# TensorE's order of the MLP's two layers inside a round: the second layer's unit ahead of the first layer's

## What is computed

```
normed = (xf - mu) / jnp.sqrt(var + 1e-05) * ln_g + ln_b
x_attn = normed @ attn_w.T + attn_b + xf
h = jnp.einsum('meti,ehi->meth', tok, fc1_w) + fc1_b[None, :, None, :]
h = jax.nn.gelu(h, approximate=False)
y = jnp.einsum('meth,edh->metd', h, fc2_w) + fc2_b[None, :, None, :]
out = jax.nn.gelu(yf @ next_w.T + next_b, approximate=False)
```

## Time and profile before

| | us |
|---|---|
| median of 3 runs | 179.08 |
| the three runs | 178.96, 179.08, 179.25 |
| the profiled execution, its own time | 178.95 |
| its span, first to last instruction | 177.2 |
| PE busy | 166.2 (94%) |
| DVE busy | 131.4 (74%) |
| ACT busy | 94.7 (53%) |
| POOL busy | 93.3 (53%) |

### The profile page before, as it was taken

One profiled execution on the slowest core, in us unless ns is written; L12 is line 12 of the kernel. 1 busy time (PEld: TensorE's weight loads), 2 busy tenths in 40 slices (PEclk: granted clock), 3 DMA queues, 4 the chain that ended last, 5 costly groups with the idle time before them and its releaser, 6 DMA issues.

```text
span 177.2 us, 3381 instructions
## 1 busy us (share of the span) xinstructions
PE 166.2 (94%) x1129; PEld 134.6 (76%) x1129; DVE 131.4 (74%) x406; ACT 94.7 (53%) x220; POOL 93.3 (53%) x153
## 2 busy tenths in 40 slices
PE   5987999999999999988999989999999999998992
PEld 2575776587654679856557889999999999987891
DVE  4889973785430496899875798989989897658983
ACT  3048992342223322201435765977769597786691
POOL 4227673599920000120401495896978969698600
PEclk9999999999999999999999999999999999999999
DMA  4995000000000000000000000010010100101103
GB/s 141 372 433 235 4 0 4 4 0 0 0 0 0 0 4 0 0 2 4 0 0 0 0 4 0 0 61 4 0 59 2 63 0 6 57 4 59 42 21 118
DMA packets 2326, 7.53 MB, mean 42 GB/s; under 512 B 255, under 2 KB 893, under 8 KB 2053
## 3 DMA queue, kind: packets, MB, share of 16 engines
q1 hardware_dynamic: 2162, 7.18, 10.5%
q10 hardware_dynamic: 146, 0.13, 0.2%
HBM read 5.22 MB, written 2.10 MB: 41 GB/s over the span
## 4 chain that ended last, share of the span: by engine, by line
PE 68%; DVE 10%; POOL 8%; ACT 6%; issue 5%; DMA 1%; ACTq 0%; DVEq 0%; POOLq 0%
PE bank L1184 10%; PE bank L1204 9%; PE bank L1134 7%; PE bank L995 6%; PE bank L1054 6%; PE bank L1048 5%; PE bank L1131 4%; PE bank L944 3%; PE bank L1154 3%; DVE u L713 2%; PE bank L1019 2%; POOL hid_p L472 2%; PE bank L971 2%; POOL rstd L455 2%; PE bank L1161 1%
## 5 line engine op out<-in xcount | busy, mean ns | idle before, releaser
L472 POOL TENSOR_TENSOR hid_p<-hid_f,hid_p 128x256 fp32r<-128x256 f32 x52 | 37.2, 739 | 17.8 <-ACT hid_p L605 16.2
L603 ACT ACTIVATE hid_f<-bank,pa 128x256 f32<-128x256 f32 x64 | 30.7, 488 | 17.5 <-PE bank L1184 15.7
L1184 PE MATMUL bank<-xaT_p,fc_p 128*128 128x256 f32 x192 | 35.1, 293 | 0.2 <-issue 0.2
L1204 PE MATMUL bank<-hid_p,out_hi 128*128 128x256 f32 x128 | 33.0, 292 | 1.4 <-POOL hid_p L472 1.2
L455 POOL TENSOR_TENSOR rstd<-spread,neg_half 128x8 f32<-128x8 f32 x8 | 13.2, 1646 | 37.3 <-DVE spread L849 37.3
L1184 PEld LDWEIGHTS bank<-xaT_p,fc_p 128*128 128x128 f32 x192 | 26.7, 189 | 0.3 <-issue 0.3
L1204 PEld LDWEIGHTS bank<-hid_p,out_hi 128*128 128x128 f32 x128 | 23.3, 187 | 3.2 <-POOL hid_p L472 2.4
L605 ACT ACTIVATE hid_p<-bank,pa 128x256 fp32r<-128x256 f32 x48 | 23.4, 487 | 0.0
L1134 PE MATMUL bank<-pb,xh 128*128 128x128 f32 x128 | 19.5, 275 | 0.0
L1204 PE MATMUL bank<-hid_p,out_lo 128*128 128x256 f32 x64 | 17.8, 278 | 0.0
L693 DVE BATCH_NORM_STATS2 st<-h 128x6 f32<-128x128 f32 x64 | 13.9, 279 | 4.5 <-ACT h L530 4.2
(11 more groups left out here) (130 smaller groups left out, 341.5 us busy)
## 6 DMA issues: line engine op xcount, KB each, us to landing
fc_w<-in_fc SPq DMA_DIRECT2D x2, 2048.0 KB, 11.2
out<-res SPq DMA_DIRECT2D x7, 256.0 KB, 2.0
pa<-in_pack_a SPq DMA_DIRECT2D x1, 407.0 KB, 3.2
pb<-in_pack_b SPq DMA_DIRECT2D x1, 320.0 KB, 4.4
out<-res SPq DMA_DIRECT2D x2, 128.0 KB, 1.7
pc<-in_pack_c ACTq DMA_DIRECT2D x1, 128.5 KB, 2.3
pw<-in_pack_a SPq DMA_DIRECT2D x1, 64.0 KB, 4.0
emb_w<-in_emb SPq DMA_DIRECT2D x1, 62.5 KB
```

The source lines that it names most:

```text
L472: nc.gpsimd.tensor_tensor(hid_p[1][:, half, c, :], hid_f[:, m % HID_SLOTS, :], hid_p[0][:, half, c, :].bitcast(F32), ALU.subtract).then_in ...
L603: full = nc.scalar.activation(hid_f[:, m % HID_SLOTS, :], src, ACT.Gelu, bias=bias)
L1184: last = mm(fc1_bank(8 * b + n)[:, 0:HALF], fc1_p[w][:, e * HID + c * P:e * HID + (c + 1) * P], xaT_p[m][:, b % 2, half, :], start=(k == 0 ...
L1204: last = mm(out_bank(b, half)[:, half * HALF:(half + 1) * HALF], out_p[w][:, e, c * CH:(c + 1) * CH], hid_p[m][:, half, c, :], start=(c == ...
```

## The change

Inside a place, `out_part` of the older unit now always stands ahead of `fc1_part`. Before, that was so only at place 3; at the seven others `fc1_part` was first. The number of instructions, their waits, and the queues of the other engines stay as they were.

```diff
-                        if n == LAG - 1 and j >= 1:
+                        if 8 * j + n >= LAG:
                             out_part(8 * j + n - LAG)
                         fc1_part(j, n)
-                        if n != LAG - 1 and 8 * j + n >= LAG:
-                            out_part(8 * j + n - LAG)
```

## The result

The changed kernel takes 183.05 us (median of 4 runs, 182.64 to 183.54) against 179.02 us before (4 runs, 178.71 to 179.25). The ratio is 1.0232 with a 95% interval of 1.0215 to 1.0249: 4.0 us slower, where 4.1 (183.2) was forecast.

The account below looks back on a forecast made before the run. Two bounds at once: TensorE's own work and a loop through ACT, DVE and POOL, less than 0.1 us apart. Terms 0.35 + 2.60 + 0.30 + 0.10 + 0.70 = 4.05 us gave 183.2, range 181.5 to 184.0.

Parts of the forecast that it names:

- Step 1: Place 1, rounds 1 to 5: first layer's unit 1 runs 0.35 us later, so copy L619 is 0.30 to 0.35 late.
- Step 2: Place 7: first layer's unit 7 now follows the wait for POOL's low part, 0.35 us more before the next mixer.
- Step 3: Place 4: Gelu L581 comes later and TensorE waits for it; place ends 0.70 us later, alone about 0.55 a round.
- Step 4: Where it applies: round 0 costs 0.35 us, rounds 1 to 4 2.60, round 5 0.30, unit 6.2 about 0.1.
- Step 5: Round 7: L603 of unit 7.2 starts 0.74 us later, behind unit 6.6's third matmul; 0.70 counted.
- The unknown at the end: Copy of 6.6's high part, 1.38 us during POOL's addition: shifted times could return up to 1.1 us or add as much.
- (d): Rival: the copy of 6.6 slips from under POOL's addition, total 182.1 us; chance 0.07.

Follow-up runs that it names:

- The two faster kernels: Against the kernel before: first layer's unit 1 and transpose_xa earlier, 178.06 us; that plus first layer's unit 2 earlier, 177.78 us.

## Why the prediction was right

Laid along the two traces, the terms of the sum are these (us). The marks are the timelines' starts of L1131 and L455, the end of unit 6.6's L472, and the start of unit 7.7's third matmul, the last of all:

| stretch | before | after | more | forecast |
|---|---|---|---|---|
| round 0, mixer to mixer | 10.62 | 10.99 | 0.37 | 0.35 |
| rounds 1 to 4 | 42.59 | 45.19 | 2.60 | 2.60 |
| round 5 to POOL's power for sequence 7 | 7.33 | 7.63 | 0.30 | 0.30 |
| from there to the end of unit 6.6's low part | 13.27 | 13.37 | 0.10 | 0.10 |
| from there to the last third matmul | 5.64 | 6.36 | 0.72 | 0.70 |
| sum | | | 4.09 | 4.05 |

**Step 1** holds: place 1 alone costs 0.29 a round, the copy is 0.29 late. The smaller value (ACT against the transposes, 0.05 apart) was the right one.

**Step 2** holds: place 7 alone costs 0.35 a round in the mean. It is in series with step 1: 10.99, 10.95 and 11.26 for 7, 1 and both.

**Step 3** was right in its mechanism. The next unit behind place 4 starts 8.11 after the round's mixer (136.31 in the timeline after), exactly as worked out (134.17 less 126.06). Its size was off: alone it costs 0.45 and not the 0.55 of the text, since I counted only one of the two short waits that it swallows. (The text's own subtraction, 0.70 less 0.1, gives 0.60, as the expectation has it.) In the full change this didn't matter, because the loop was longer anyway, 0.65 a round, by more margin than I knew.

**Step 4** holds for rounds 0 to 5 (0.37, 2.60 and 0.30), but its last term, 0.10 for unit 6.2 of the first layer in the gap between two waits, is right by luck. The two runs that exchange place 2 in round 6 too (places 2 and 4; places 2, 4 and 7) take 13.28 from the power to the end of unit 6.6's low part, as good as the 13.27 before: that exchange costs nothing. The wait for unit 5.7's low part takes it up: TensorE starts unit 6.3 of the first layer 7.42 behind the power in the trace after and 7.44 before. In the trace after, POOL too keeps the distances of before (10.13 and 10.12 behind the power) up to one subtraction, which is drawn 0.85 long where it had 0.74. First before, then after:

```profile
164.82 0.74 POOL L472 TENSOR_TENSOR hid_p<-hid_f,hid_p 128x256 fp32r<-128x256 f32 x1 [0.89 <-DVE hid_p L778]
168.55 0.85 POOL L472 TENSOR_TENSOR hid_p<-hid_f,hid_p 128x256 fp32r<-128x256 f32 x1 [0.89 <-DVE hid_p L778]
```

That is the whole 0.10 of the table. Why it is longer in this one profiled execution is open; none of the nine experiments shows it (0.73 to 0.75). Without this term the sum would have been 3.95 and not 4.05.

**Step 5** holds. Place 2 of round 7 alone costs 0.78 in the median, and the last stretch is 0.72 longer in the table, where 0.70 was taken.

**The unknown at the end** did not come into play. The copy of 6.6's high part starts at 169.60, while POOL's addition (169.36, drawn 1.48) runs, as before:

```profile
L778 DVE CAST hid_p<-hid_f x12: 278/291/1386, 163.5 to 177.4; 128x256 fp32r<-128x256 f32 x12
```

The longest is 1.386, against 1.382 in the earlier trace rows. So (d) was not the case. In the nine experiments the longest copy takes 1.375 to 1.387 as well, so no run moved the two against each other, and what (d) would have given stays untested. The median in the earlier trace rows hides that this copy is not the only slow one: two others, back to back from 159.43 to 161.26, are drawn 1.09 and 0.82 long in the trace before.

## What to carry to other kernels

An engine that is busy for the whole of a round may still not be the only bound: follow one round through the other engines and see whether the loop comes back just in time. Where it does, the order of two neighbours on the busy engine has a price: the length of what now stands ahead of the unit that feeds the loop (less the slack there, 0.05 here), plus the length of what now stands between the wait that closes the loop and its next turn. The exchanges at places 0, 5 and 6, and at place 2 of round 6, do neither and were free. Waits in series add, waits beside one another don't; which is which could be read ahead of time here by asking whether the second one's releaser hangs on the first.

## What I had not expected of the hardware

That "busy for 10.66 of 10.66" hid about 0.25 us of waiting in each round: 0.15 around the projection and 0.1 at the third matmul of unit 3. Matmuls are drawn overlapping, so waits this short leave no gap; they show only as a distance between starts (0.91 instead of 0.81 behind L1154) or as a matmul drawn 0.39 long where its neighbours have 0.28. The two faster kernels got back only the wait at the third matmul (unit 3's group to the next mixer takes 0.35 in their round 3, against 0.48 before); around L1154 both still show the 0.91.
